# A transformer block on one Trainium2 core: the low halves of the GELU on GpSimd, and the transposes of the normalised tokens by DMA

## What is computed

```python
x = x + xattn(layernorm(x), ctx, ctx)   # 16 heads of 32, 257 context tokens for each sequence
x = x + attn(layernorm(x))              # one causal head; softmax over ALL (t, s) pairs of a sequence
x = x + ffn(layernorm(x))               # 512 -> 2048 -> 512, gelu, weights alpha * sign(w)

def attn(x):
    q, k, v = x @ Wq + bq, x @ Wk + bk, x @ Wv + bv
    scores = where(causal, q @ k.T / sqrt(512), -1e30)
    e = exp(scores - max(scores, axis=(-2, -1)))
    return (e / sum(e, axis=(-2, -1))) @ v

def ffn(x):
    h = gelu(x @ (alpha1 * sign(w1)).T + b1)
    return h @ (alpha2 * sign(w2)).T + b2
```

## Time and profile before

| | us |
|---|---|
| three runs, median (lowest to highest) | 2730.92 (2727.81 to 2732.71) |
| the profiled execution: time / span | 2726.66 / 2724.9 |
| TensorE busy | 2603.2 (96%) |
| VectorE busy | 1683.2 (62%) |
| ScalarE busy | 1250.7 (46%) |
| GpSimd busy | 776.1 (28%) |

### The profile page before, as it was taken

How to read it: one execution, slowest core, us unless ns; L and a number is a source line. 1 busy time by engine, 2 the same in 40 slices (tenths; PEclk the granted TensorE clock), 3 DMA queues, 4 the chain that set the end, 5 groups by cost and what they waited for, 6 DMA issues and landing times. The chain is left out here.

```text
span 2724.9 us, 51525 instructions
## 1 busy us (share of the span) xinstructions
PE 2603.2 (96%) x16820; PEld 1512.2 (55%) x16820; DVE 1683.2 (62%) x3520; ACT 1250.7 (46%) x2766; POOL 776.1 (28%) x1530
## 2 busy tenths in 40 slices
PE   7999999999999999999999999976899899989999
PEld 3555555555555555555555555533666566556666
DVE  7555656555555555555655565547676766766675
ACT  4345554445544454445444544423344444434444
POOL 2233433333333333333333333310211211111110
PEclk9999999999999999999999999987999999999999
DMA  4234433443333333333333333323000000000000
GB/s 143 99 84 106 104 90 90 97 98 82 82 86 92 83 82 85 89 88 82 82 89 90 82 82 87 70 68 116 16 16 17 31 15 15 31 15 15 16 24 16
DMA packets 344619, 187.76 MB, mean 69 GB/s; under 512 B 290672, under 2 KB 311152, under 8 KB 344048
## 3 DMA queue, kind: packets, MB, share of 16 engines
q1 hardware_dynamic: 344560, 187.00, 27.5%
HBM read 109.06 MB, written 8.65 MB: 43 GB/s over the span
## 5 line engine op out<-in xcount | busy, mean ns | idle before, releaser
L712 DVE TENSOR_TENSOR e_lo<-e,e_hi 128x1024 f16<-128x1024 f32 x128 | 156.8, 1225 | 413.9 <-ACT e_hi L640 413.9
L797 PE MATMUL psum<-c_hi,xWk_hi 128*128 128x512 f16 x1024 | 388.4, 379 | 2.3 <-PEq L140 2.3
L797 PE MATMUL psum<-xWv_hi,c_hi 128*128 128x512 f16 x1024 | 389.2, 380 | 0.0
L797 PE MATMUL psum<-xWv_lo,c_hi 128*128 128x512 f16 x1024 | 389.1, 380 | 0.0
L797 PE MATMUL psum<-xWv_hi,c_lo 128*128 128x512 f16 x1024 | 388.9, 380 | 0.0
L797 PE MATMUL psum<-c_lo,xWk_hi 128*128 128x512 f16 x1024 | 388.4, 379 | 0.0
L797 PE MATMUL psum<-c_hi,xWk_lo 128*128 128x512 f16 x1024 | 388.4, 379 | 0.0
L122 POOL TENSOR_TENSOR c_lo<-ctx_raw,c_hi 128x1024 f16<-128x1024 f32 x128 | 272.2, 2127 | 335.3 <-ACT c_hi L618 325.0
L633 ACT ACTIVATE e<-psum,neg_max 128x257 f32<-128x257 f32 x512 | 235.8, 474 | 280.8 <-DVE neg_max L693 280.8
L704 DVE SCALAR_TENSOR_TENSOR v_lo<-psum,v_hi 128x512 f16<-128x512 f32 x256 | 177.0, 691 | 249.8 <-ACT v_hi L626 249.8
L570 POOL COPY bd_hi<-heads_hi 32x128 f16 (+1 forms) x512 | 152.9, 299 | 575.4 <-PE psum L797 553.0
(11 more groups left out here) (224 smaller groups left out, 5586.8 us busy)
## 6 DMA issues: line engine op xcount, KB each, us to landing
ctx_raw<-in_ctx_main SPq DMA_DIRECT2D x128, 512.0 KB, 3.6
xs<-in_x SPq DMA_DIRECT2D x8, 1024.0 KB, 5.7
v_rep<-v_last_rows SPq DMA_DIRECT2D x512, 16.0 KB, 1.7
xb<-in_x SPq DMA_DIRECT2D x16, 512.0 KB, 3.4
out<-res_out SPq DMA_DIRECT2D x32, 256.0 KB, 2.1
ffn_raw<-in_w_t SPq DMA_DIRECT2D x11, 512.0 KB, 3.4
late_raw<-in_late_w SPq DMA_DIRECT2D x4, 1024.0 KB, 4.8
res<-in_w_t SPq DMA_DIRECT2D x5, 512.0 KB, 3.6
```

The source lines that it names most:

```text
L712: nc.vector.tensor_tensor(e_lo[:, :, :], e[:, :, 0:S], e_hi[:, :, :], ALU.subtract).then_inc(e_lo_done, 1)
L797: mm = nc.tensor.matmul(bank, a, b, start=(n == 0), stop=(n == len(steps) - 1))
```

## The change

1. `gelu_lo` of all 256 steps is made by GpSimd and no longer by VectorE. GpSimd's other work is cut up and put between these: `stage_heads` in two calls, `stage_input` and `res += b2` by tiles of 128x512.
2. The normalised tokens are split before they are turned: ScalarE casts `xn` to `xn_hi` (fp16, SBUF), VectorE makes `xn_lo`, and SP turns both by one DMA transpose each (128x1024 fp16) into `x2T` or `x3T`, whose layout is now tile by tile. The 16 fp32 matmuls of the transposes in a round go, and so does their PSUM.
3. The projection stands behind F(6) and no longer behind F(5), scores and values behind F(8), weights times values behind F(12). `xn_hi` of the second norm stands behind F(3) on ScalarE.
4. SP's rounds are written out one by one and no longer loop. The two bias tiles `bk_wide_hi` and `bk_wide_lo`, used once at the start, lie in `x3T_hi` now.

```diff
@@ SP
+            def turn2(n):
+                turn(n, 2, s["val_ps"], T * n, x2T_hi, x2T_lo, s["x2T_landed"])
+            def turn3(n):
+                turn(n, 3, s["h_ps"], NJ * n, x3T_hi, x3T_lo, s["x3T_landed"])
+            def turn(n, k, free, count, hi, lo, landed_sem):
+                past(sp, free, count)
+                for source, done, dst in ((xn_hi, s[f"xn_hi{k}_done"], hi), (xn_lo, s[f"xn_lo{k}_done"], lo)):
+                    sp.wait_ge(done, T * (n + 1))
+                    sp.dma_start_transpose(dst.rearrange("p t c n -> p (t c) n"),
+                                           source.rearrange("p t d -> p (t d)")).then_inc(landed_sem, 16)
...
                 if has_tail(n):
                     store(n - 2)
-                if not (isinstance(n, int) and (n >= NG - 1 or n == 0)):
+                if n < NG - 1 and n > 0:
                     load(n + 1)
+                if front:
+                    turn2(n)
+                    turn3(n)
@@ GpSimd
+            def hidden(g, j):
+                pool.wait_ge(s["gelu_hi_done"], NJ * g + j + 1)
+                nc.gpsimd.tensor_tensor(act_lo[j % AR][:, :], act[j % AR][:, :], act_hi[j % AR][:, :],
+                                        ALU.subtract).then_inc(s["gelu_lo_done"], 1)
+            def add_b2(n, u, t):
+                pool.wait_ge(s["norm3_done"], T * n + t + 1)
+                nc.gpsimd.tensor_tensor(res[u][:, t, :], res[u][:, t, :], b2_row[:, :],
+                                        ALU.add).then_inc(s["b2_added"], 1)
...
+                F(0)
+                if front:
+                    power(n, s["eps2_done"], s["rstd2_done"])
+                F(1)
+                if following:
+                    stage_heads(n + 1, (heads_hi, at_hi))
+                F(2, 3)
+                if following:
+                    stage_heads(n + 1, (heads_lo, at_lo))
+                F(4, 5, 6)
+                if following:
+                    stage_input(n + 1, 0)
+                F(7, 8)
+                if following:
+                    stage_input(n + 1, 1)
+                F(9, 10, 11, 12)
+                if front:
+                    power(n, s["eps3_done"], s["rstd3_done"])
+                F(13, 14)
+                if front:
+                    add_b2(n, u, 0)
+                F(15)
+                if front:
+                    add_b2(n, u, 1)
@@ ScalarE
+            def high_xn(n, k):
+                past(eng, s["x3T_landed" if k == 2 else "x2T_landed"], 32 * (n if k == 2 else n + 1))
                 for t in range(T):
-                    eng.wait_ge(bank_ready, T * n + t + 1)
-                    nc.scalar.copy(dst[:, :, t * P:(t + 1) * P], chunks(g_bank(t), KC)).then_inc(done, 1)
+                    eng.wait_ge(s[f"norm{k}_done"], T * n + t + 1)
+                    nc.scalar.copy(xn_hi[:, t, :], xn[:, t, :]).then_inc(s[f"xn_hi{k}_done"], 1)
...
-                F(0, 1, 2, 3, 4)
-                if front:
-                    high_T(s["t2_ps"], x2T_hi, s["x2T_hi_done"], n)
-                F(5)
+                F(0, 1, 2, 3)
+                if front:
+                    high_xn(n, 2)
+                F(4, 5, 6)
...
-                F(*range(8, NJ))
-                if front:
-                    past(eng, s["h_ps"], NJ * n)
-                    high_T(s["t3_ps"], x3T_hi, s["x3T_hi_done"], n)
+                F(*range(9, NJ))
+                if front:
+                    high_xn(n, 3)
@@ VectorE
+            def low_xn(n, k):
                 for t in range(T):
...
+                    dve.wait_ge(s[f"xn_hi{k}_done"], T * n + t + 1)
+                    nc.vector.tensor_tensor(xn_lo[:, t, :], xn[:, t, :], xn_hi[:, t, :],
+                                            ALU.subtract).then_inc(s[f"xn_lo{k}_done"], 1)
-            def hidden(g, j):
-                dve.wait_ge(s["gelu_hi_done"], NJ * g + j + 1)
-                nc.vector.tensor_tensor(act_lo[j % AR][:, :], act[j % AR][:, :], act_hi[j % AR][:, :],
-                                        ALU.subtract).then_inc(s["gelu_lo_done"], 1)
@@ TensorE
-                run(h_bank(j), [(sign1[:, k, cols], x3[:, k, :]) for k in range(KC)
+                run(chunks(h_bank(j), T), [(sign1[:, k, cols], x3[:, :, k, :]) for k in range(KC)
                                 for x3 in (x3T_hi, x3T_lo)]).then_inc(s["h_ps"], 1)
...
                 if ffn:
-                    pe.wait_ge(s["x3T_lo_done"], T * (g + 1))
-                F(0, 1, 2, 3, 4)
-                if front:
+                    pe.wait_ge(s["x3T_landed"], 32 * (g + 1))
+                F(0, 1, 2, 3, 4, 5, 6)
+                if front:
+                    pe.wait_ge(s["x2T_landed"], 32 * (n + 1))
...
-                    transposes(n, s["norm2_done"], s["t2_ps"])
-                F(5)
...
-                F(6, 7)
+                F(7, 8)
...
-                F(8, 9, 10, 11)
+                F(9, 10, 11, 12)
...
-                F(12, 13, 14, 15)
-                if front:
-                    transposes(n, s["norm3_done"], s["t3_ps"])
+                F(13, 14, 15)
```

More of the change, by code:

```diff
@@ L1076, in _ @@
             load(1)
+            turn2(0)
             stage_pieces(4, len(pieces))
-            rounds(sp, one)
+            turn3(0)
+            for n in range(1, NG + 1):
+                one(n, n % 2, n < NG, n > 0)
             store(NG - 1)
@@ L1103, in one, with F @@
             def one(n, u, front, ffn):
[L1104 to L1114, removed]
+                g = n - 1
+                following = front and not (isinstance(n, int) and n == NG - 1)
+                def F(*js):
+                    for j in js:
+                        if ffn:
+                            hidden(g, j)
+                F(0)
[22 more added lines that the diff above has]
+                    add_b2(n, u, 1)
             nc.gpsimd.memset(half[:, :], -0.5).then_inc(s["pool_const"], 1)
             pool.wait_ge(s["consts_landed"], 16 * 6)
-            stage_input(0)
+            stage_input(0, *range(T))
             nc.gpsimd.memset(zeros[:, :], 0.0).then_inc(s["pool_const"], 1)
@@ L1389, in F @@
                     for j in js:
-                        if ffn:
-                            hidden(g, j)
-                        else:
+                        if not ffn:
                             for piece_nr in SPLIT_SLOTS.get(j, ()):
@@ L1414, in one @@
                 if front:
[L1415 removed]
+                    low_xn(n, 2)
                 F(5)
@@ L1470, in run @@
                 return mm
-            def transposes(n, norm_done, done):
-                for t in range(T):
-                    pe.wait_ge(norm_done, T * n + t + 1)
-                    for c in range(KC):
-                        mm = nc.tensor.transpose(chunks(g_bank(t), KC)[:, c, :], xn[:, t, c * P:(c + 1) * P],
-                                                 ident[:, :])
-                    mm.then_inc(done, 1)
             def layer1(g, j):
@@ L1569, in one @@
                             m = 2 * r + c
[L1570 to L1571 removed]
+                            mm = run(chunks(chunks(g_bank(Y_BANK[r]), 2)[:, c, :], T),
+                                     [(w[:, k, m * P:(m + 1) * P], xt[:, :, k, :]) for k in range(KC)
                                       for w, xt in passes(m_hi, m_lo, x2T_hi, x2T_lo)])
                         mm.then_inc(s["y_ps"], 1)
[L1574 removed]
+                F(7, 8)
                 if front:
@@ L1578, in one @@
                         rows = slice(t * P, (t + 1) * P)
-                        mm = run(sc_bank[:, t, :], [(q[:, m, rows], k[:, m, rows]) for m in range(KC)
+                        mm = run(sc_bank[:, t, :], [(q[:, m, rows], k[:, t, m, :]) for m in range(KC)
                                                     for q, k in passes(y_hi, y_lo, x2T_hi, x2T_lo)])
@@ L1582, in one @@
                     for t in range(T):
-                        rows = slice(t * P, (t + 1) * P)
-                        run(g_bank(2 + t), [(xt[:, k, rows], w[:, k, :]) for k in range(KC)
+                        run(g_bank(2 + t), [(xt[:, t, k, :], w[:, k, :]) for k in range(KC)
                                             for xt, w in passes(x2T_hi, x2T_lo, *late["sWv"])]
                             ).then_inc(s["val_ps"], 1)
-                F(8, 9, 10, 11)
+                F(9, 10, 11, 12)
                 if front:
```

53 lines of the change are left out of this document (20 added, 33 removed).

## The result

| | before | after |
|---|---|---|
| median (lowest to highest), us | 2729.86 (2727.81 to 2732.71), 4 runs | 2663.39 (2663.07 to 2664.31), 4 runs |
| profiled execution: time / span | 2726.66 / 2724.9 | 2663.45 / 2661.7 |
| TensorE / VectorE busy | 2603.2 / 1683.2 | 2571.4 / 1584.6 |
| ScalarE / GpSimd busy | 1250.7 / 776.1 | 1249.2 / 980.8 |

A forecast was written before the change was run, and what follows sets the result against it. TensorE bounds, with a 4.0 us hole per round; 46.1 + 1.85 + 0.5 + 0.25 = 48.7 against 52.95, times 14 = 59.5, with edges net 56.5, giving 2675 us; own range 2662 to 2690, whole range 2648 to 2712.

The forecast's parts named there:

- The bound and the hole: Token stages: TensorE bounds, with a 4.0 us hole per round from VectorE standing still while GpSimd stages; both end together.
- TensorE's floor of 46.1: Token round: TensorE's bare work is about 47.8 us with the fp32 transposes and 46.1 without them.
- The waits at steps 0, 1, 2 and 13: FFN steps where gelu_lo on GpSimd isn't hidden: TensorE waits 0.25, 0.7, 0.4 and 0.5, together 1.85 us a round.
- x2T: Second norm's DMA transpose: lands at 18.4 to 19.6, due at 18.7; wait 0 to 0.9, taken as 0.5 us.
- x3T: Third norm's DMA transpose: lands 11.1 to 12.1 after weights times values, due at 12.6; hidden by Wo, 0.25 us added.
- Rival A: Token rounds: low halves at 0.5, xn_lo never held, waits of 1.2, rounds of 47.3; total 2653; chance 17%.
- Round 0: First round: projection waits one landing longer, 3 us more, bounded by 0 and 4; weight pieces behind the transposes waited anyway.
- Round 1 and the last: Edges: round 1 gains 4 us; round 16, with no Wo to hide the x3T chain, loses 4.
- The clock: TensorE's clock: no stretch at 1.2 GHz, 1.00 in nearly all rounds; that gain is already in the 52.95.
- B: Port dearer: VectorE's two-input instructions wait for GpSimd, x2T lands 1.5 us later, clock falls; round 51.1, total 2710; 17%.
- C: Slower: paired transposes serialise on one queue at 4.9 us each, x2T and x3T late; round 58, total 2800; 6%.
- D: No net change: the hole isn't the port but something that stays, new waits eat the 1.74; total 2731; 4%.

The follow-up runs named there:

- experiment 3: Kernel before, plus one wait: GpSimd holds the next group's staging until x2T_lo is done; 2661.95 us, ratio 0.9750.
- experiment 8: Changed kernel with the projection on TensorE one FFN step earlier, behind step 5, in all rounds; 2717.04 us, ratio 0.9953.
- experiment 9: Changed kernel with the projection on TensorE and ScalarE's copies of y both one FFN step earlier; 2690.68 us, ratio 0.9857.
- experiment 10: Kernel of experiment 5 with the third norm's tokens of round 15 transposed by TensorE, split from PSUM by ScalarE and VectorE; 2644.48 us, ratio 0.9688.
- experiment 4: Changed kernel with round 0's first transposes issued on SP ahead of the waiting weight piece and the next input load; 2655.88 us, ratio 0.9728.
- experiment 2: Changed kernel with gelu_lo back on VectorE and GpSimd's staging in one piece as before; 2741.53 us, ratio 1.0045.
- experiment 6: Kernel of experiment 2 with SyncE's order of experiment 4 and the next group's staging held until xn_lo is done; 2676.07 us, ratio 0.9804.
- experiment 5: Kernel of experiment 4 with the old places of projection, scores, values and weights times values in round 0 only; 2651.17 us, ratio 0.9715.
- experiment 11: Kernel of experiment 5 with GpSimd's staging moved back behind low halves 5, 6, 7 and 8; 2645.46 us, ratio 0.9689.
- experiment 12: Kernel of experiment 5 with the pieces of experiments 10 and 11 together; 2640.58 us, ratio 0.9673.

## Why the prediction was right, and where not

*The bound and the hole: right, and shown.* One wait on GpSimd's staging (experiment 3) takes the hole away with all else in place. One reading is loose: VectorE's stretched work ends at 2231.22 and GpSimd's at 2230.26, 1 us apart and not together; no term hangs on it.

*TensorE's floor of 46.1: right.* The round of 47.38, less the 1.33 counted above, is 46.05.

*The waits at steps 0, 1, 2 and 13: right in place, too large in size.* Against 0.25, 0.7, 0.4 and 0.5 stand 0.33, 0.47, 0.25 and 0.18: step 0 cost a little more, the others less. The low half itself was 0.67 for the 0.65 taken (0.77 as a mean with the stretched ones). The rule of the Trainium skill (GPSIMD Engine Reference, section 4.1), about twice VectorE's time, is not borne out for this form: 0.67 against 0.43 is a factor of 1.6.

*x2T: chain right, wait too large.* On the round's clock `power` ends at 11.4 (11.5 was said), the two `xn` at 13.5 (13.9), `xn_lo` at 15.6 (15.3 to 16.4), the landing is at 18.5 (18.4 to 19.6). The due time moved with the smaller waits in front to 18.4, so 0.1 is left of the 0.5. Experiments 8 and 9 show that there is no margin behind it.

*x3T: right.* It lands 11.1 behind the end of weights times values (11.1 to 12.1) and is due at 12.3; the 0.25 added was nothing.

The mis-sized term is thus the sum of the waits of a round, 2.6 against 1.33: for nearly each I took the value towards the dear end. That makes 14 x 1.27 = 18 of the 20 us. Rival A had this round almost exactly (waits of 1.2, 47.3) at 17%.

*Round 0: wrong, -16.8 for -3.* The step that failed is "SP's pieces of weights behind the first transposes were waiting anyway". I looked at what stands behind the transposes on SyncE and not at what stands ahead of them: a piece that waits for a free place, and a load of 512 KB. The moved places were taken as free there as well, while a slot of round 0 holds weight pieces and waits. Rival A had the same fault, which is why its 2653 is 10 us too low, though its round was right. That 2663 fell into the forecast's own range of 2662 to 2690 is therefore in part luck: with round 0 as forecast, the true rounds would have given some 2650, in rival A's place. The bottom of the whole range is also misnamed: rounds at the floor of 46.1 would give 2636 with rival A's edges, and not 2648.

*Round 1 and the last: right*, +5.7 and -5.0 for +4 and -4, the latter shown by experiment 10.

*The clock: right.* Rounds 2 to 14 took 53.3 before and 47.3 now, 6.0 less. Of that, 1.74 are the transposes, 3.0 the waits (4.33 before, counted by starts in the earlier trace rows, and 1.33 now), and 1.2 the clock (what 53.3 is over the 52.12 of a round at full clock), 5.9 together.

*Rivals B, C, D:* landings in rounds 2 to 15 are at 2.8, `y_lo` and `val_lo` kept their 0.69, and the clock didn't fall.

What the prediction did not see at all: neither engine had to be relieved. A staging step moved by one line gives 2661.95, the same as the whole change within the measurement. And of the two parts, the transposes alone are a loss: 5.8 us gained in rounds 2 to 15, some 20 lost in round 0 and at the end.

## What to carry to other kernels

When two engines stretch each other, ask first whether the work that does the stretching can run somewhere else in the round: one wait was worth as much here as moving 16 instructions and 16 transposes. A part of a change can be worth nothing or less until another removes the wait that hides it, so test each alone and together. When a step gets onto a queue, read what is ahead of it there, and cost the first and the last round by themselves: they are other programs, and 23 us lay in them and in one order of staging.

## What the runs showed of the hardware

- GpSimd's subtraction 128x256 fp32 to fp16 takes 0.67 us undisturbed (VectorE 0.43), up to 1.21 beside VectorE.
- A cast on VectorE from one SBUF tensor is held as well: `y_hi` 1.14 for 0.43 while GpSimd added to `xb` (experiment 3).
- A DMA transpose 128x1024 fp16 inside SBUF took 1.23 to issue and 2.8 to land; behind two loads of 512 KB 4.38 and 6.5 (the changed kernel, round 0), and ahead of them 1.23 again (experiment 4).
- With one pause of 3.6 us a round TensorE's clock was 0.97 and 0.94 in two rounds (experiment 2), and 0.97 and 1.00 by turns in the kernel before. With one of 1.2 (experiment 6) or 1.6 (experiment 9) it was 1.00 in the stretches read, 1960 to 2060 and 2170 to 2610 us.
- Open: in several variants' profiles (the rounds of experiments 5, 6, 8, 9, 11 and 12) one round between 2082 and 2166 us is longer by 0.6 to 2.8 us. In experiment 9 (both steps moved) the issue of `x2T_lo` took 2.40 there instead of 1.23 and the landing was late. What else the DMA engines did then was not looked into.
